# Row maxima of cross attention taken over two PSUM banks by one reduction

## The reference, cut to what matters

```
q = split_heads(q_in @ Wq.T); k = split_heads(mem @ Wk.T); v = split_heads(mem @ Wv.T)
scores = einsum('bhqd,bhkd->bhqk', q, k) / sqrt(16)
attn = softmax(where(mem_mask, scores, -inf), axis=-1)
out = einsum('bhqk,bhkd->bhqd', attn, v)
```

## Time and profile before

| | us |
|---|---|
| three runs | 2035.58, 2063.30, 2073.66 (median 2063.3) |
| profiled execution | 2037.29, span 2035.5 |
| cross attention, first to last maximum | 972.9 to 1539.6 |
| mean granted TensorE clock | 0.934 |

### The profile page before, as it was taken

How to read it: one execution, slowest core, us unless ns; L and a number is a source line. 1 busy time by engine, 2 the same in 40 slices (tenths; PEclk the granted TensorE clock), 3 DMA queues, 4 the chain that set the end, 5 groups by cost and what they waited for, 6 DMA issues and landing times.

```text
span 2035.5 us, 32048 instructions
## 1 busy us (share of the span) xinstructions
PE 1880.9 (92%) x11708; PEld 990.3 (49%) x11708; DVE 1408.5 (69%) x2838; ACT 1157.4 (57%) x2252; POOL 370.3 (18%) x573
## 2 busy tenths in 40 slices
PE   7698999999999999987899999999999859999994
PEld 2244333333333333324544444444443648888883
DVE  6464999999999999616889999999992550000003
ACT  1022777778777777763067777777778403322221
POOL 8014122222222222120000000000000012333321
PEclk9795999999999999978589999999999859999997
DMA  7240000001100000002000100101000144656664
GB/s 251 107 148 31 21 32 26 27 26 31 36 33 28 26 27 26 2 12 109 26 17 27 33 31 27 38 23 40 25 22 2 42 140 136 203 170 196 182 171 119
DMA packets 79910, 135.58 MB, mean 67 GB/s; under 512 B 11332, under 2 KB 57053, under 8 KB 78141
## 3 DMA queue, kind: packets, MB, share of 16 engines
q1 hardware_dynamic: 60466, 102.14, 15.2%
q0 software_dynamic: 9024, 12.17, 3.2%
q10 hardware_dynamic: 10264, 19.22, 2.5%
HBM read 103.74 MB, written 29.11 MB: 65 GB/s over the span
## 4 chain that ended last, share of the span: by engine, by line
PE 79%; DVE 12%; DMA 4%; issue 3%; ACT 1%; POOL 0%; ACTq 0%; POOLq 0%; SPq 0%; DVEq 0%
PE banks L933 22%; PE banks L883 17%; PE banks L921 16%; PE banks L1130 8%; PE banks L1142 7%; DVE skip L1389 4%; PE banks L819 2%; DVE CM L1385 2%; DVE CM L1383 2%; PE banks L809 1%; PE banks L1024 1%; DMA kxD<-parts 1%; PE banks L894 1%; PE banks L813 1%; DMA oper<-slD 1%
## 5 line engine op out<-in xcount | busy, mean ns | idle before, releaser
L1223 ACT ACTIVATE XT<-banks 128x512 f32<-128x512 f32 x1240 | 658.8, 601 | 242.4 <-PE banks L921 208.8
L883 PE MATMUL banks<-oper 52*128 52x512 f32 (+1 forms) x2048 | 730.7, 440 | 40.8 <-DMA oper<-slD 17.5
L921 PE MATMUL banks<-oper 54*128 54x512 f32 x1856 | 658.1, 456 | 15.9 <-POOL oper L697 10.5
L1383 DVE TENSOR_REDUCE CM<-banks 128x1 f32<-128x402 f32 x1024 | 524.3, 569 | 29.0 <-PE banks L883 19.3
L883 PEld LDWEIGHTS banks<-oper 52*128 52x128 f32 x2048 | 349.6, 192 | 301.7 <-DVE CM L1383 173.8
L921 PEld LDWEIGHTS banks<-oper 54*128 54x128 f32 x1856 | 289.3, 187 | 296.7 <-ACT XT L1223 171.9
L1223 ACT ACTIVATE late<-banks 128x512 f32<-128x512 f32 x616 | 327.7, 601 | 90.8 <-PE banks L921 76.5
L933 PE MATMUL banks<-XT,VS 128*32 128x256 f32 (+1 forms) x3584 | 365.2, 480 | 1.6 <-ACT XT L1223 0.9
L1599 DVE TENSOR_SCALAR YS<-banks,gs 128x256 f32<-128x256 f32 x46 | 22.3, 484 | 311.5 <-PE banks L1142 311.5
L1294 ACT ACTIVATE HID<-banks,b1E 128x256 f32<-128x256 f32 x184 | 77.1, 470 | 225.4 <-PE banks L1130 225.4
L933 PE MATMUL banks<-late,VS 128*32 128x256 f32 (+1 forms) x1784 | 181.4, 479 | 0.3
(11 more groups left out here) (185 smaller groups left out, 1178.3 us busy)
## 6 DMA issues: line engine op xcount, KB each, us to landing
W<-in_w1T_dram SPq DMA_DIRECT2D x23, 1024.0 KB
W<-in_w2T_dram SPq DMA_DIRECT2D x23, 1024.0 KB, 5.7
oper<-kD SPq DMA_DIRECT2D x31, 256.0 KB
oper<-kxD SPq DMA_DIRECT2D x32, 208.0 KB
qD<-parts ACTq DMA_DIRECT2D x8, 512.0 KB, 3.6
kD<-parts ACTq DMA_DIRECT2D x8, 512.0 KB, 2.8
qxD<-parts ACTq DMA_DIRECT2D x8, 512.0 KB, 3.2
oper<-qxD SPq DMA_DIRECT2D x32, 128.0 KB
```

Source lines behind the costliest of these rows:

```text
L883: mm = pe.matmul(slot[:, n * QB:n * QB + ch], QO[64 * g:64 * g + M_ROWS, c2, col:col + P], KO[64 * g:64 * g + M_ROWS, c2, k0:k0 + ch], sta ...
L921: pe.matmul(bank, KO[64 * g:64 * g + S_ROWS, c, b * P:(b + 1) * P], QO[64 * g:64 * g + S_ROWS, c, q0:q0 + QB], start=True, stop=True).then ...
L1223: act.activation(PT[(c * plan.nu + u) % PRING], S[(c * plan.nu + u) % SBANKS], ACT.Exp).then_inc(A.exps, 1)
L1383: dve.tensor_reduce(CM[:, a, b:b + 1], slot[:, 0:ch], AX.X, ALU.max).then_inc(A.freed, 1)
```

## The change

Two neighbouring items of kind "max" of cross attention, numbers 2k and 2k + 1 of the ring, go into two banks side by side (3 and 4, or 5 and 6). VectorE no longer waits for the even one. It waits for the odd one, takes both maxima with one reduction over 2 x 402 elements, and frees two numbers. The two results go to two columns of `CM` that may lie far apart; which of the two products goes to the lower bank is chosen so that the step between the columns is positive (`pair_slots`). In block 2 the "sum" item moves from behind the five fills to ahead of them. Self attention is not touched: its plan has `causal` true, and there the old order and the old reduction stay.

```diff
+    def place(self, a, b):
+        return a * 4 + b
+
+    def pair_slots(self, item, turn):
+        n = self.table.index((item[1], item[2]))
+        mine, other = self.place(*self.table[n]), self.place(*self.table[n ^ 1])
+        return (turn // 2 * 2 + int(mine > other)) % self.slots, min(mine, other), max(mine, other)
...
         if b == SUM_AT and not (whole and h == 0):
-            items += self.wide(("sum", 0, 0, -1, None))
+            total = self.wide(("sum", 0, 0, -1, None))
+            items = items + total if self.causal else total + items
...
-                    slot = R[bank % plan.slots]
+                    slot = R[plan.pair_slots(item, bank)[0] if kind == "max" and not alibi else bank % plan.slots]
...
-                    dve.wait_ge(A.filled, pos + 1)
+                    paired = kind == "max" and not alibi
+                    if not paired or bank % 2:
+                        dve.wait_ge(A.filled, pos + 1)
...
-                        if not alibi:
-                            dve.tensor_reduce(CM[:, a, b:b + 1], slot[:, 0:ch], AX.X, ALU.max).then_inc(A.freed, 1)
+                        if paired:
+                            if bank % 2:
+                                at, lo, hi = plan.pair_slots(item, bank)
+                                two = banks[:, (SBANKS + at // 2 * 2) * QB:(SBANKS + at // 2 * 2 + 2) * QB]
+                                dve.tensor_reduce(CM[:, :, :].rearrange("p t b -> p (t b)")[:, lo:hi + 1:hi - lo],
+                                                  two.rearrange("p (s n) -> p s n", s=2)[:, :, 0:ch], AX.X, ALU.max).then_inc(A.freed, 2)
```

## The result

The changed kernel is slower: three runs of 2141.68, 2153.53 and 2159.37 us, median 2153.5, against 2063.3 before. The ratio is 1.0498 with a 95% interval of 1.03 to 1.0696. In later rounds it was 1.0531 (1.0466 to 1.0596). The ratios leave out runs that a lower clock disturbed, the medians do not. I had forecast 2099 with a range of 2065 to 2136: right in sign, outside the range in size.

What follows compares the result with a forecast made beforehand. TensorE was taken to set the pace, VectorE nearly co-limiting. Terms of 1.7, 1.1 and 0.4 us a cycle gave 45 us over 14 cycles; with 4 us before the heads, 2050 + 49 = 2099 us, range 2065 to 2136.

Steps and rivals of the forecast that it cites:

- What bounds the kernel: Cross attention at full clock: TensorE sets the pace, busy the whole window, with VectorE busy 96% of it.
- Part 1, the instruction: Cross-attention maxima: a pair's reduction takes 0.989 us against 1.138 for two; real relief 0.063 us a pair, worth nothing beside TensorE.
- the 75 us that I gave as a sign: Sign that the forecast was right: VectorE's busy time over the kernel falls by about 75 us.
- Part 2, the pairs: Ordinary key blocks: the loop from odd fill to reusing even fill takes 1.52 us, too long; costs 1.7 us a cycle.
- Part 3, the sum: Block with the sum moved ahead of its fills: fills wait for pairs that began late; costs 1.1 us a cycle.
- Part 4, the head's end: After a head's last maximum: the small-instruction chain follows a longer reduction, returning the next pair later; +0.4 us a cycle.
- Part 5, before the heads: Before the heads, 88 products at reducer pace and half clock: two pairs take 2.15 us against 1.93; 4 us in all.
- Sum: Whole kernel: 3.2 us a cycle, 45 us over 14 cycles, with 4 us before the heads makes +49 us.
- The clock, put at nothing: Rival, chance 0.08: the clock falls in the heads, six heads in a mixed clock, 60 us more, 2159 us.
- my own bounds: Bounds on the cost: 28 to 70 us for the 14 cycles, -3 to +6 us before the heads.
- VectorE is the pace: Rival, chance 0.06: VectorE sets the pace in the heads, so pairs save 3.4 us a cycle; 47 us less, 2003 us.
- hidden handoff: Rival, chance 0.16: ordinary blocks lose nothing, 1.5 us a cycle stay; 21 us more, 2071 us, within 2%.

Runs made afterwards that it cites:

- the loop cut to 1.1 us: Changed kernel with the pair's reduction reading only the first 201 columns of each product; 35.5 us a cycle, 2042.1 us for the whole kernel.
- the kernel with longer maxima: Kernel before plus a second reduction of 40 columns ahead of each cross-attention maximum; 39.5 us a cycle at full clock, 2249.9 us in all.
- late start: Kernel before with the sum ahead; VectorE waits for the odd product, then takes two single maxima, freeing each bank separately; 36.4 us a cycle.
- late release: Kernel before with the sum ahead; each maximum taken when its product is in, both banks freed together after the odd one; 36.3 us a cycle.

## Why the prediction was wrong in size

Two steps failed. The cycle's sum was too small, 3.2 us for 4.16; and the clock, which I held at 1.00 in the heads, had no term at all. With the first put right, and 3 us for head 0, which my sum left out, the forecast would have been 2050 + 65 = 2115 us, still inside the range. The clock took it out.

**What bounds the kernel:** right. TensorE set the pace, and taking work from VectorE gave nothing: with the loop cut to 1.1 us the cycle is 35.5.

**Part 1, the instruction:** 0.993 us measured, 0.989 forecast. The page's busy time counts overlapping reductions once, so it fell by 28.5 us, near 512 x 0.063 = 32; the 75 us that I gave as a sign was wrong.

**Part 2, the pairs:** the mechanism, its place and its signs were right, the size was not. Ten ordinary blocks lost 2.18 us, where I had 1.7; two blocks lost 0.46 (5.71 against 5.25), where I had 0.33. The loop's parts were 0.45, 1.00 and 0.05 us, and the first of them, fill to reduction, was taken from single reductions as 0.385. This 0.06 us stands in series with every wait, and two waits in two blocks make most of the missing 0.13 (an estimate). I had named this latency as what would make the number wrong first.

**Part 3, the sum:** 0.06 us alone. With pairs the two blocks round it lost 1.64 us, where I had 1.1. By moving it to block 3 some 0.6 us came back, so a good part belongs to the pairs anywhere around a sum.

**Part 4, the head's end:** 0.34 us measured, 0.4 forecast.

**Part 5, before the heads:** 3.1 us measured for 64 of the 88 products, 4 forecast for all. The other 24 lie in head 0, which took 4 us more at the same clock; that its own blocks wait as those of a cycle do had no term.

**Sum:** some 65 us of work and waiting against 49, 13 of the difference in the cycles and 3 in head 0.

**The clock, put at nothing:** that was the rival that I gave 8% and left outside the range. My reason was that TensorE waits 0.5 us at each head's end before and the clock stays at 1.00; but the change was forecast to add 3.2 us of waits to each cycle, and about that the trace of before says nothing. So it does not stand beside the forecast as another case: the waits that I forecast come with a risk to the clock. In the three profiles of the changed kernel the fallen clock took 22, 22 and 5 us of the 14 cycles. Of the 116 us between the first two profiles, 65 are work and waiting, 22 the head at half clock, 3 a slower clock in head 0 and 31 the stretch behind the last maximum, less 5 ahead of the first. The 31 are not the change's as far as is known: one of two profiles of before has them too. The rival's own number, 2159 us, lies close to the 2153.5 measured, but partly by luck: it had six heads in a mixed clock, 10 us each, where there was one at half clock, and the rest of the loss lay outside the heads. The range should have held waits and clock together. Its upper end was also narrower than my own bounds: 70 us for the cycles and 6 before the heads above 2074 are 2150, and not 2136.

**Other rivals.** *VectorE is the pace* and *hidden handoff* are out.

I had cited the Trainium skill, "TensorE: Matmul & The Clock Gate", section on psum-queue depth-cycling, for short idles between groups that make the clock alternate; the traces agree, clearest the kernel with longer maxima at 0.54 to 1.00.

## What to carry to other kernels

Batching n buffers into one instruction saves its fixed part, but it also turns a ring of n x k slots into one of k: write down the loop from the last fill of a batch to the first fill that reuses it, and compare it with the distances in the order of the engine that sets the pace. If it doesn't fit, put the fills of a batch side by side. Count a wait of the matrix engine twice, once for itself and once for the clock, and take more than one profile of a kernel before a stage's difference is put down to a change.

## What the runs showed of the hardware

- A late start costs 1.0 us a cycle, a late release 0.9, both 4.2: over the ten ordinary blocks of a cycle they lose 0.5, 0.0 and 2.3. Waits add up only beyond the slack, so halves tried alone say little of the whole.
- A reduction over two groups in two banks starts 0.06 to 0.07 us later behind its fill (0.45 and 0.54 us) than one within a bank (0.37 to 0.38 and 0.48), whether it is 0.57 or 0.99 us long. One over 1024 adjoining columns in two banks does not: it starts 0.04 us behind the end of its fill, as single ones do.
- VectorE work of 0.19 us ahead of each of 64 maxima made a cycle 4.1 us longer at full clock, 58 us in all, but the kernel 10% slower, and its mean clock fell to 0.863 from 0.928 and 0.934.
- A reduction of 402 columns takes 0.569 us but follows the one before it by 0.483: merging two saves 0.063 us of pace and not the 0.15 that the durations show.
- Code that does not differ takes 496 or 525 us behind the last maximum, in profiles of the same kernel, as its clock over the first 85 us is 0.94 or 0.56.
- In the late-start kernel TensorE was busy without a break for 181.8 us, and the mean granted clock was 0.51.
